# A two-layer transformer stack on one core: the written-out order of every engine redone, the experts' down products two pieces behind in the bank of the turns, and the last batch finished in halves

## The chip, the cores and the metric

The kernel runs on one core of a Trainium2 chip. Its time is the device time of one execution in microseconds (us). The core has five engines with a queue of instructions each: TensorE (PE in the rows; its weight loads are shown apart as PEld), VectorE (DVE), ScalarE (ACT), GpSimd (POOL) and SyncE (SP). An engine executes its queue in order, and waits on semaphores that the others raise. SP issues most of the transfers.

## The reference

The input x is (4, 512, 128) float32: four batches of 512 tokens, width 128. Two layers follow each other:

```
x = L0_attn_x
for L in (0, 1):
    xn = layernorm(x)
    s = attention_L(xn)            # L=0: 16 heads, window of 64, softmax of scores scaled by a "fitness"
                                   # L=1: windows of 64 blended, out projection, then a dense MLP (128-512-128)
    g = silu(experts_L(xn))        # each token goes to one of 8 experts, 128-512-128
    x = x + s * g                  # L=0: erf-gelu between the products; L=1: relu
```

## The kernel before

**What the pieces are.** The attention of a batch is cut into eight units. In layer 0 a unit is first scored (`scores0`), ScalarE takes the tanh of the scores (L906), and VectorE reduces the scores and the tanh (`reduce0`, L1197 and L1200); after the eighth unit the fitness of the batch is known (`inverse`, `inverse_sum`, `fitness`, `turn_fitness`, `spread_fitness`, `fit_q`), and a period later the same units run once more as `logits0`, exp on ScalarE (L915), `weigh0`, `turn_back`, `normalise_head`, `turn_head0`, `project_out`, `keep_out0`. Layer 1 has the same two passes (`scores1`, `reduce1`; `logits1`, `weigh1`, `blend`, `turn_head1`, `project_out`, `keep_out1`), and then the dense MLP (`mlp_stats`, `mlp_norm`, `mlp_turn`, `mlp_up`, `mlp_hidden`, `mlp_down`, `mlp_out`).

**The experts.** The tokens are sorted by expert: GpSimd scatters the rows of `xn` into `sorted_x` in DRAM with 16 indirect transfers (L1456). The sorted rows are 24 tiles of 128, worked in pairs: 12 groups per layer, `g` = 0 to 11 for layer 0 and 12 to 23 for layer 1. Of each group SP loads two blocks of weights and 256 rows (`load`), TensorE transposes the rows into bank ED of `ps_turn` (`pe_turn`), ScalarE copies them out (`act_turn`, L366), TensorE multiplies by the first weights into banks EX and ED (`pe_up`, eight products recorded as 16 instructions, L349), VectorE adds the bias (`vec_bias`, L385), ScalarE applies gelu or relu (`act_hidden`, L371), TensorE multiplies by the second weights (`pe_down`, also 16 instructions, L358), ScalarE copies out (`act_out`, L377), GpSimd adds the bias (`pool_bias`, L392) and SP stores. The weights and rows live in a ring of two groups. When a layer's groups are done, the rows are gathered back (`gather`, L1463), and `join` adds s * g to x.

**What sets the order.** Each engine's program is written out by hand as ten periods of eleven steps. at(p, k) is step k of period p. In period p batch p-1 is scored and batch p-2 is weighed in layer 0, batch p-5 and p-6 likewise in layer 1, and batch p-7 goes through the MLP. `u` is k-3, the unit of the second pass. GROUP_AT says in which step a group is turned and multiplied up. In the step of group g the order was:

- TensorE: `pe_turn(g)`; `logits`, `turn_back`; `scores`; `project_out`; projections of the next batch; `inverse_sum`, `turn_fitness`, `spread_fitness`; `values`; `pe_up(g)`; the MLP; `weigh`, `turn_head`; and in the step after, as its last work, `pe_down(g)` into bank EX.
- ScalarE: `act_turn(g)`; exp; tanh; copies; `act_hidden(g)`; and at the end of the step after, `act_out(g)`.
- VectorE: `normalise_head`/`blend`; `reduce0`/`reduce1`; `keep_out`; the norm of the next batch; the fitness; joins; the MLP; `vec_bias(g)` last.
- SP: `store(g)` two steps after the group's step, and right behind it `load(g + 2)`.

Single PSUM banks are handed on by `Bank.take`: whoever wants bank M (shared by the projections, the values, the spread norms, the turned heads and the MLP) waits on PE until the last holder's result has been read by VectorE or ScalarE. The packing of q and k for a batch (`pack0`, `pack1`, L299) is 12 transfers on SP for q and 12 for k, and that of the fitted q (`pack_fit`) is 18.

## Time and profile before

| | us |
|---|---|
| median of 3 runs | 671.32 (670.61 to 672.29) |
| the profiled execution | 669.64 |
| its span, first to last instruction | 667.8 |
| TensorE busy | 486.0 (73%) |
| VectorE busy | 329.9 (49%) |
| ScalarE busy | 259.6 (39%) |
| GpSimd busy | 125.1 (19%) |
| mean granted TensorE clock | 0.761 of full |

A busy time is the sum of the spans of an engine's instructions. The granted clock is 1.0 at 2.4 GHz and 0.5 at 1.2 GHz; a mean between the two says how the stretch is divided between them.

### The profile page before, as it was taken

How to read it: one execution, taken by the hardware profiler on the slowest of the kernel's cores; microseconds unless marked ns; L12 is line 12 of the kernel's file. 1: busy time of each engine (PE TensorE's matmuls, PEld its weight loads, DVE VectorE, ACT ScalarE, POOL GpSimd, SP SyncE). 2: the span in 40 equal slices, each digit the busy share in tenths (PEclk: the TensorE clock that was granted, in tenths of full speed). 3: DMA queues.
4: the chain of work that ended last, by engine and by line, in shares of the span. 5: the costliest groups of instructions: out<-in, count | busy, mean ns of one | idle time of the engine just before them, and what ended most of it. 6: DMA issues, size and time to landing. Idle time of an engine off the chain costs nothing.

```text
span 667.8 us, 16301 instructions
## 1 busy us (share of the span) xinstructions
PE 486.0 (73%) x6899; PEld 357.2 (53%) x6904; DVE 329.9 (49%) x760; ACT 259.6 (39%) x349; POOL 125.1 (19%) x142
## 2 busy tenths in 40 slices
PE   3844775767676857677679768769998889877835
PEld 2723554646455634434445346547587767764723
DVE  5756855374524664878473567245222623321151
ACT  3114314456544642362143232115641465347112
POOL 6437000000000002132212110711000110027010
PEclk9556788788968886595676665558897999898758
DMA  8631657355722355115452150266323534312010
GB/s 243 165 58 60 214 167 152 104 118 130 158 91 88 98 77 74 19 36 76 72 73 43 27 77 3 65 192 153 97 90 99 162 111 130 95 61 53 14 48 16
DMA packets 49552, 63.57 MB, mean 95 GB/s; under 512 B 9396, under 2 KB 41012, under 8 KB 49460
## 3 DMA queue, kind: packets, MB, share of 16 engines
q1 hardware_dynamic: 46440, 55.97, 35.3%
q0 software_dynamic: 3040, 6.56, 3.8%
q8 instruction: 54, 0.88, 0.6%
q14 instruction: 18, 0.15, 0.1%
HBM read 38.33 MB, written 8.26 MB: 70 GB/s over the span
## 4 chain that ended last, share of the span: by engine, by line
PE 38%; DVE 20%; issue 16%; SPq 9%; ACT 6%; POOL 6%; DMA 5%; ACTq 0%; POOLq 0%; DVEq 0%
SPq L299 6%; POOL sorted_x L1456 4%; PE ps_turn L349 4%; PE ps_turn L358 4%; DMA xg<-sorted_x 4%; PE ps_proj L768 3%; PE ps_proj L617 2%; PE ps_score L697 2%; PE ps_score L760 2%; PE ps_proj L742 2%; DVE tsum L1200 2%; PE ps_proj L610 2%; PE ps_score L725 2%; DVE gm L1197 2%; SPq L326 1%
## 5 line engine op out<-in xcount | busy, mean ns | idle before, releaser
L915 ACT ACTIVATE pT<-ps_score 128x1024 f32<-128x1024 f32 x64 | 65.6, 1025 | 28.6 <-PE ps_score L725 16.4
L392 POOL TENSOR_TENSOR ys<-ys,wblock 128x256 f32<-128x256 f32 x24 | 17.4, 725 | 310.9 <-ACT ys L377 310.9
L1290 DVE TENSOR_REDUCE gm<-ps_score 128x16 f32<-128x1024 f32 x32 | 39.1, 1221 | 63.0 <-PE ps_score L697 62.9
L1197 DVE TENSOR_REDUCE gm<-ps_score 128x8 f32<-128x1024 f32 x32 | 39.1, 1222 | 62.6 <-ACT pT L906 62.5
L358 PE MATMUL ps_turn<-wblock,xn 128*128 128x128 f32 x384 | 57.8, 313 | 12.1 <-ACT xn L371 12.1
L358 PEld LDWEIGHTS ps_turn<-wblock,xn 128*128 128x128 f32 x384 | 54.0, 224 | 17.4 <-ACT xn L371 15.7
L349 PE MATMUL ps_turn<-xgT,wblock 128*128 128x128 f32 x384 | 58.5, 316 | 0.3 <-ACT xgT L366 0.3
L349 PEld LDWEIGHTS ps_turn<-xgT,wblock 128*128 128x128 f32 x384 | 55.3, 229 | 2.6 <-issue 1.7
L371 ACT ACTIVATE xn<-xn 128x1024 f32<-128x1024 f32 x24 | 25.3, 1055 | 58.9 <-DVE xn L385 58.9
L906 ACT ACTIVATE pT<-ps_score 128x1024 f32<-128x1024 f32 x32 | 32.6, 1020 | 39.0 <-PE ps_score L554 38.8
L385 DVE TENSOR_TENSOR xn<-ps_turn,wblock 128x512 f32<-128x512 f32 x48 | 31.9, 685 | 14.7 <-PE ps_turn L349 14.2
L933 ACT ACTIVATE headT<-ps_proj 128x128 f32<-128x128 f32 x32 | 8.8, 276 | 77.0 <-PE ps_proj L631 41.4
L1200 DVE TENSOR_REDUCE tsum<-pT 128x8 f32<-128x1024 f32 x32 | 38.7, 1208 | 0.0
L1309 DVE RECIPROCAL wtot<-ps_proj 128x32 f32<-128x32 f32 x16 | 5.7, 357 | 66.7 <-PE ps_proj L617 66.7
L1456 POOL DMA_INDIRECT sorted_x<-xn,pos x32 | 30.9, 965 | 41.3 <-DVE pos L1152 32.1
L924 ACT ACTIVATE ctxT<-ps_proj 128x512 f32<-128x512 f32 x32 | 19.1, 598 | 43.7 <-PE ps_proj L742 23.5
L610 PE MATMUL ps_proj<-pT,v 128*32 128x256 f32 x256 | 26.4, 489 | 11.3 <-DVE head L1255 11.3
L1463 POOL DMA_INDIRECT moe<-sorted_y,pos x32 | 30.7, 959 | 21.2 <-DMA sorted_y<-ys 12.3
L742 PE MATMUL ps_proj<-pT,v 128*18 128x64 f32 x1024 | 25.4, 249 | 9.5 <-DVE xsT L1313 9.5
L617 PE MATMUL ps_proj<-first,ctxT 128*128 128x128 f32 x128 | 25.6, 332 | 6.5 <-ACT ctxT L924 6.4
L742 PEld LDWEIGHTS ps_proj<-pT,v 128*18 128x18 f32 x1024 | 19.1, 112 | 18.5 <-issue 13.6
L524 PE MATMUL ps_proj<-rmsn,spread 128*128 128x128 f32 x64 | 14.5, 398 | 12.5 <-DVE rmsn L1182 10.6
(294 smaller groups left out, 964.1 us busy)
## 6 DMA issues: line engine op xcount, KB each, us to landing
wblock<-in_L_we SPq DMA_DIRECT2D x48, 578.0 KB, 4.5
qT<-xs SPq DMA_DIRECT2D x48, 64.0 KB
xg<-sorted_x SPq DMA_DIRECT2D x24, 128.0 KB, 5.6
sorted_y<-ys SPq DMA_DIRECT2D x24, 128.0 KB, 1.8
q2raw<-xn SPq DMA_DIRECT2D x48, 64.0 KB
eq<-xs SPq DMA_DIRECT2D x36, 64.0 KB
ek<-xl SPq DMA_DIRECT2D x36, 64.0 KB
sorted_x<-moe POOLq DMA_DIRECT2D x2, 768.0 KB, 8.5
```

The source lines that it names most:

```text
L299: eng.dma_start(dst[r:r + HD, :, :], parts[64 * par:64 * par + 64, s, :]).then_inc(loaded, 16)
L349: ins = te.matmul(bank[:, c * P:(c + 1) * P], w1[:, 2 * (g % 2) + n, c * P:(c + 1) * P], xgT[:, n, :], start=True, stop=True)
L358: ins = te.matmul(EX[:, n * P:(n + 1) * P], hT[:, n, c * P:(c + 1) * P], w2[:, 2 * (g % 2) + n, c * D:(c + 1) * D], start=(c == 0), stop=( ...
L610: ins = te.matmul(o, v0[b % 2][:, u, 32 * g:32 * g + 32], pT[:, n % 2, par * 512 + hf * 256:par * 512 + hf * 256 + 256], start=True, stop= ...
L617: ins = te.transpose(CT[:, j * P:(j + 1) * P], ctxT[:, j * P:(j + 1) * P], ident)
L742: ins = te.matmul(o, v[:, b % 2, m, 18 * h:18 * h + 18], pT[:, n % 2, 64 * h:64 * h + 64], start=True, stop=True)
L906: nc.scalar.activation(th[:, n % 2, :], SLOT[PLACE["p1", 0, b, n]], ACT.Tanh, scale=0.5).then_inc(f.th, 1)
L915: nc.scalar.activation(pT[:, n % 2, :], SLOT[PLACE["p2", L, b, u]], ACT.Exp).then_inc(s.p, 1)
L1197: nc.vector.tensor_reduce(gmx[b % 2][:, t, :].rearrange("p (a r) -> p a r", a=2)[:, :, 4 * hf:4 * hf + 4], SLOT[PLACE["p1", 0, b, n]].rear ...
L1200: nc.vector.tensor_reduce(tsum[:, t, :].rearrange("p (a r) -> p a r", a=2)[:, :, 4 * hf:4 * hf + 4], th[:, n % 2, :].rearrange("p (a j k) ...
L1290: nc.vector.tensor_reduce(gm[:, b % 2, :].rearrange("p (a m r) -> p a m r", a=2, m=NU)[:, :, m, :], SLOT[PLACE["p1", 1, b, m]].rearrange(" ...
L1456: po.indirect_dma_start(out=sorted_x, out_offset=bass.IndirectOffsetOnAxis(ap=pos[:, t:t + 1], axis=0), in_=xn[:, t * D:(t + 1) * D], in_o ...
```

## The change

It changes when each piece of work stands in each engine's queue, and very little of what is computed.

- **Groups of layer 0** stand one place earlier in GROUP_AT: the first at step (1,4) instead of (1,6), the last at (3,4) instead of (3,6). Their first loads are at (1,1) instead of (1,2).
- **Rows and weights** are loaded by two functions with two semaphores. `pe_turn` waits for the rows alone, `pe_up` for the weights. The rows of group g+2 are asked for in the step after group g's, once it is turned; the weights of g+2 three steps after g's step, behind `store(g)`.
- **`pe_down(g)`** moves from the end of the step after to the step two after, right behind `pe_turn(g+1)`, and writes columns 256 to 511 of ED, the bank whose columns 0 to 255 hold the turned rows. `act_turn` now waits for the down product before as well.
- **TensorE's step** becomes: `spread_fitness`; `logits`, `turn_back`; `project_out`; `inverse_sum`, `turn_fitness`, `turn_max`; `pe_turn`; `pe_down`; `scores`; projections; `values` (layer 0's at k = 3 instead of 2); `pe_up`; the MLP; `weigh`, `turn_head`.
- **ScalarE's step**: exp; `act_turn(g)`; `act_out(g-1)`; tanh; copies; and `act_hidden(g)` near the end of the step after.
- **VectorE's step**: `vec_bias` of the step before comes first, then `normalise_head`/`blend`, the norm of the next batch (`mean_square`, `rms_inverse` and `normalise` at k = 3, 4, 5 and 6), `keep_values0`, `split_in`, `mlp_out` (at k = 10 instead of 9), the fitness, `keep_out`, and only then `reduce0`/`reduce1`. The `bn_stats` of the MLP move from `mlp_stats` into `keep_out1`, one with each tile.
- **The end**: the four last tanh stand together at (10,0) and write to `xrT` instead of the single tile `tj`; the joins of layer 1 stand together at (10,4), behind `mlp_norm` of the last batch. Batches 0 to 2 are joined as before. For batch 3 the join is made of what is known before the down product of the MLP, and `last_out` adds that product in two halves, one from bank M and one from EX, each followed by its own output transfer.
- **GpSimd**: `mlp_root` and `mlp_bias` stand ahead of `pool_bias` in their step; the last gathers are two steps later in the list. **SP**: the output transfers stand behind the loop.

The diff, cut to its core:

```diff
-GROUP_AT = [at(1, 6), at(1, 8), at(1, 10), at(2, 1), at(2, 3), at(2, 5), at(2, 7), at(2, 9), at(3, 0), at(3, 2), at(3, 4), at(3, 6),
+GROUP_AT = [at(1, 4), at(1, 6), at(1, 8), at(1, 10), at(2, 1), at(2, 3), at(2, 5), at(2, 7), at(2, 9), at(3, 0), at(3, 2), at(3, 4),
-FIRST_LOADS = {at(1, 2): 0, at(7, 0): 1}
+FIRST_LOADS = {at(1, 1): 0, at(7, 0): 1}
...
             def pe_turn(self, te, g, turn_bank):
-                te.wait_ge(self.loaded[g % 2], 48 * (g // 2 + 1))
+                te.wait_ge(self.rows_in[g % 2], 16 * (g // 2 + 1))
...
                 te.wait_ge(self.kept, g + 1)
+                te.wait_ge(self.loaded[g % 2], 32 * (g // 2 + 1))
...
-            def pe_down(self, te, g, up_bank):
+            def pe_down(self, te, g, turn_bank, beside_turn):
                 te.wait_ge(self.hidden, g + 1)
-                up_bank.take(te, self.y, g + 1)
+                if beside_turn:
+                    turn_bank.held = (self.y, g + 1)
+                else:
+                    turn_bank.take(te, self.y, g + 1)
...
-                        ins = te.matmul(EX[:, n * P:(n + 1) * P], hT[:, n, c * P:(c + 1) * P],
+                        ins = te.matmul(ED[:, (2 + n) * P:(3 + n) * P], hT[:, n, c * P:(c + 1) * P],
...
                     ac.wait_ge(self.up, 2 * g)
+                    ac.wait_ge(self.down, g)
...
+                if c == B - 1:
+                    exb.take(te, m1.out, c + 1)
                 for t in range(NT):
+                    o = (EX if c == B - 1 and t >= 2 else M)[:, t * D:(t + 1) * D]
...
-                    if s in GROUP:
-                        ex.pe_turn(te, GROUP[s], edb)
...
+                    if s in GROUP:
+                        ex.pe_turn(te, GROUP[s], edb)
+                    if s - 2 in GROUP:
+                        ex.pe_down(te, GROUP[s - 2], edb, s in GROUP)
...
-                    if s - 1 in GROUP:
-                        ex.pe_down(te, GROUP[s - 1], exb)
...
-                    if s in GROUP:
-                        ex.act_hidden(ac, GROUP[s])
...
                     if s - 1 in GROUP:
-                        ex.act_out(ac, GROUP[s - 1])
-                    if s in LAST_JOIN:
-                        join_tanh(1, LAST_JOIN[s])
+                        ex.act_hidden(ac, GROUP[s - 1])
+                    if s == at(10, 0):
+                        for n in range(B):
+                            join_tanh(1, n)
...
+            def last_out():
+                for h in range(2):
+                    lo = (B - 1) * T + h * 2 * D
+                    dv.wait_ge(m1.dn, 2 * B - 1 + h)
+                    st(nc.vector.scalar_tensor_tensor(out=s_out[:, lo:lo + 2 * D], in0=(M, EX)[h][:, h * 2 * D:(h + 1) * 2 * D], scalar=0.5,
+                                                      in1=moe[:, lo:lo + 2 * D], op0=ALU.mult, op1=ALU.mult))
+                    nc.vector.tensor_tensor(x[:, lo:lo + 2 * D], x[:, lo:lo + 2 * D], s_out[:, lo:lo + 2 * D], ALU.add).then_inc(j_x, 1)
...
+                    if s - 1 in GROUP:
+                        ex.vec_bias(dv, GROUP[s - 1])
...
-                    if s in GROUP:
-                        ex.vec_bias(dv, GROUP[s])
-                    if s in LAST_JOIN:
-                        join(1, LAST_JOIN[s])
+                    if s == at(10, 4):
+                        for n in range(B):
+                            join(1, n)
+                        last_out()
...
-                    if s - 2 in GROUP:
-                        g = GROUP[s - 2]
+                    if s - 3 in GROUP:
+                        g = GROUP[s - 3]
                         ex.store(sp, g)
                         if g % NG + 2 < NG:
-                            ex.load(sp, g + 2)
+                            ex.load_weights(sp, g + 2)
+                    if s - 1 in GROUP and GROUP[s - 1] % NG + 2 < NG:
+                        g = GROUP[s - 1]
+                        sp.wait_ge(ex.turned, g + 1)
+                        ex.load_rows(sp, g + 2)
```

## Rows read from the trace of the kernel before

**Rows 1.** The page: busy time, share of the span and instructions of each engine.

```profile
PE 486.0 (73%) x6899; PEld 357.2 (53%) x6904; DVE 329.9 (49%) x760; ACT 259.6 (39%) x349; POOL 125.1 (19%) x142
```

**Rows 2.** Busy time by stage: stretch, length, engines, clock, DMA share, GB/s.

```profile
98.00:179.00 81.00, 58.36 (x658) 44.42 (x657) 43.49 (x73) 44.46 (x56) 4.34 (x6) 0.85 0.58 136
179.00:250.00 71.00, 47.85 (x539) 36.26 (x541) 36.05 (x57) 34.84 (x44) 2.89 (x4) 0.85 0.37 90
250.00:321.00 71.00, 50.29 (x538) 28.59 (x535) 49.60 (x117) 26.48 (x35) 18.92 (x17) 0.64 0.37 54
...
480.00:545.00 65.00, 57.86 (x1051) 47.74 (x1044) 25.11 (x53) 26.39 (x41) 5.91 (x7) 0.89 0.39 117
```

**Rows 3.** The waits of TensorE: total us, times, longest.

```profile
PE ps_turn L358 <- ACT xn L371: 12.1, 9, 3.9
PE ps_proj L610 <- DVE head L1255: 11.3, 7, 3.9
PE ps_turn L341 <- DMA xg<-sorted_x: 11.3, 8, 2.7
PE ps_proj L500 <- DVE rmsn L1174: 11.1, 3, 5.2
PE ps_proj L524 <- DVE rmsn L1182: 10.6, 4, 5.2
...
PE ps_proj L742 <- DVE xsT L1313: 9.5, 7, 2.6
...
PE ps_proj L629 <- DVE s_out L1321: 6.1, 4, 2.3
PE ps_proj L495 <- DVE s_out L1262: 5.9, 2, 3.0
```

**Rows 4.** The timeline of period 1: start, us, engine, line, operation [idle before].

```profile
54.91 0.31 PE L500 MATMUL ps_proj<-second,xnT 128*64 128x32 f32 x1 [2.76 <-DVE rmsn L1174]
...
59.53 0.61 PE L542 MATMUL ps_score<-masks 64*128 64x512 bf16 x2
...
64.71 1.49 SPq L327 DMA_DIRECT2D wblock<-in_L_we  x2
...
65.92 2.08 PE L524 MATMUL ps_proj<-rmsn,spread 128*128 128x128 f32 x8 [5.19 <-DVE rmsn L1182]
...
71.90 0.69 PE L341 MATMUL ps_turn<-first,xg 128*128 128x128 f32 x2 [0.77 <-DMA xg<-sorted_x]
```

**Rows 5.** ScalarE's copies of an expert group: busy, mean ns, idle before.

```profile
L366 ACT ACTIVATE xgT<-ps_turn 128x256 f32<-128x256 f32 x24 | 9.2, 382 | 13.5 <-PE ps_turn L341 13.3
```

**Rows 6.** The timeline: the down products of a group, at 1.2 and 2.4 GHz.

```profile
195.31 3.31 PE L358 MATMUL ps_turn<-wblock,xn 128*128 128x128 f32 x16
...
465.28 2.05 PE L358 MATMUL ps_turn<-wblock,xn 128*128 128x128 f32 x16
```

**Rows 7.** The timeline of SP's queue in period 2: one packing of k.

```profile
158.75 8.25 SPq L299 DMA_DIRECT2D v<-xl  x12
```

**Rows 8.** The timeline of the last period.

```profile
639.15 0.77 PE L629 MATMUL ps_proj<-first,xsT 128*128 128x128 f32 x2 [2.31 <-DVE s_out L1321]
...
643.65 0.29 DVE L1321 TENSOR_TENSOR s_out<-s_out,ps_proj 128x128 f32<-128x128 f32 x1
...
646.55 0.87 DVE L1328 BATCH_NORM_STATS2 mstats<-s_out 128x6 f32<-128x128 f32 x4
...
649.20 1.12 DVE L1341 TENSOR_SCALAR sqq<-s_out,mmv,mrstd 128x128 f32<-128x128 f32 x4 [1.17 <-POOL mrstd L1489]
...
658.30 3.84 PE L768 MATMUL ps_proj<-third,q2raw 128*128 128x128 f32 x32 [0.78 <-ACT q2raw L973]
...
664.42 0.69 DVE L1166 SCALAR_TENSOR_TENSOR x<-moe,x 128x512 f32<-128x512 f32 x1
```

**Rows 9.** DMA issues on the page: KB each, median us to landing.

```profile
wblock<-in_L_we SPq DMA_DIRECT2D x48, 578.0 KB, 4.5
...
sorted_y<-ys SPq DMA_DIRECT2D x24, 128.0 KB, 1.8
```

More of the change, by code:

```diff
@@ L315, in __init__ @@
             def __init__(self):
-                self.loaded = [sem(f"x_in_ring{n}") for n in range(2)]
+                self.rows_in = [sem(f"x_rows_in_ring{n}") for n in range(2)]
+                self.loaded = [sem(f"x_weights_in_ring{n}") for n in range(2)]
                 self.turned, self.kept = sem("x_turned"), sem("x_turned_kept")
@@ L992, in scalar_program @@
                         exp(g1, 1, b1 - 1, u)
+                    if s in GROUP:
+                        ex.act_turn(ac, GROUP[s])
+                    if s - 2 in GROUP:
+                        ex.act_out(ac, GROUP[s - 2])
                     if 0 <= b0 < B and k < NU:
@@ L1154, in join @@
             def join(L, c):
-                y, s_, x_ = (z[:, c * T:(c + 1) * T] for z in (moe, s_out, x))
+                y, s_, x_, t_ = (z[:, c * T:(c + 1) * T] for z in (moe, s_out, x, xrT))
                 dv.wait_ge(j_e, B * L + c + 1)
@@ L1321, in keep_out1 @@
                 nc.vector.tensor_tensor(s_out[:, i * D:(i + 1) * D], s_out[:, i * D:(i + 1) * D], M[:, P:2 * P], ALU.add).then_inc(g1.o, 1)
+                dv.wait_ge(g1.o, NT * b + n + 1)
+                st(nc.vector.bn_stats(mstats[:, TILES[n], :], s_out[:, i * D:(i + 1) * D]))
             def mlp_stats(c):
-                dv.wait_ge(g1.o, NT * (c + 1))
-                for t in range(NT):
-                    i = c * NT + t
-                    st.beside(nc.vector.bn_stats(mstats[:, t, :], s_out[:, i * D:(i + 1) * D]))
-                st.meet()
                 for t in range(NT):
@@ L1394, in vector_program @@
                         keep_out1(b1 - 2, 1 + k)
[L1395 to L1414 removed]
+                    if 0 <= b0 < B and k == 9:
+                        turned_fitness(b0)
+                    if 0 <= b0 - 2 < B and k == 0:
+                        normalise_head(b0 - 2, 3)
+                    if 0 <= b1 - 2 < B and k == 0:
+                        blend(b1 - 2, 3)
+                    if 0 <= b0 < B and k < NU:
+                        reduce0(b0, k)
+                    if 0 <= b1 < B and k < NU:
+                        reduce1(b1, k)
+                    if 0 <= b0 < B and k == 7:
+                        inverse(b0)
                     for n in range(B):
@@ L1520, in gpsimd_program @@
                     s = at(p, k)
[L1521 to L1523 removed]
+                    if 0 <= c < B and k == 3:
+                        mlp_root(c)
+                        mlp_bias(c)
+                    if s - 2 in GROUP:
+                        ex.pool_bias(po, GROUP[s - 2])
+                    if s - 3 == GROUP_AT[NG - 1]:
                         gather(0, 0)
```

172 lines of the change are left out of this document (81 added, 91 removed).

## The prediction

> **What bounds the kernel now.** I read the page's busy shares first: TensorE is busy for 73% of the span, VectorE for 49%, ScalarE for 39% [rows 1]. No engine is full, so the question is what the fullest one waits for. The busy time by stage, cut where the periods begin, says where: in periods 2 to 4 of layer 0, 98 to 321 us, TensorE is busy for 58.4 + 47.9 + 50.3 = 156.5 of 223 us, and in 480 to 545 us, where layer 1's experts run, for 57.9 of 65 [rows 2]. Layer 0 is a lockstep of queues with some 30% of slack on TensorE; layer 1's expert stage is near TensorE's bound, and little is to be had there.
>
> The table of waits then says on what [rows 3]. The reader should see three families. (a) Results of VectorE that are short but stand in its queue behind work that is itself waiting: the rms norm (11.1 and 10.6 us) and the sum into `s_out` (6.1 and 5.9), together 33.7 us. (b) The head and blend normalisation, 11.3 + 9.5 = 20.8 us. (c) The experts' own chain: 12.1 us for the gelu or relu before the down product, 11.3 us for rows from DRAM.
>
> Two ends remain. At the front the experts can't start before the scatter has landed: SP issues the first loads at 64.7, and the first turn is at 71.9 [rows 4]. At the back, TensorE has only the last batch's chain to carry, so everything between 632 us and the end counts in full [rows 8].
>
> **The change part by part.** All sums are made against the profiled execution, 669.64 us, which lies 1.7 below the median of 671.32.
>
> *1. VectorE's short results ahead of the reduces, and TensorE's readers of them later.* In the old order `mean_square`, `rms_inverse` and `keep_out` wait in line behind a reduce that waits for the tanh of the same step. In the new order they are done in that idle time. The instructions are the same; what goes is the wait. Of the 33.7 us I take off 2.8 + 5.2 = 8.0 that lie in period 1 [rows 4], since that period is bound by other things (point 5). Of the 25.7 left TensorE saves at least nothing and at most all. I take 22: the result moves forward by a whole reduce pair and `values0` a step back, more than any single wait of this family is long (5.2 at most). The smaller rows of the same kind are left out of the sum, as a reserve. Bounds: 8 to 26.
>
> *2. Head and blend ahead of the norm and the reduces.* 20.8 us of waits. Here the input itself comes late, through context copy and `turn_back`, so only VectorE's own queue time goes, and `vec_bias` now stands in front of it. I take 9; bounds 0 to 20.
>
> *3. Down product two steps behind, rows apart.* The down product has a full step more for bias and gelu: of 12.1 us I take 9. The rows no longer wait for two blocks of weights (578 KB in all, 4.5 us to landing, [rows 9]): of 11.3 us I take 6, because the first rows of each layer still wait for the scatter. Bounds for both together: 5 to 23.
>
> *4. The end.* The first joins of layer 1 stand in VectorE's queue ahead of the sum that TensorE needs. At 639.15 TensorE has waited 2.31 us for that sum, which itself takes 0.29; with 0.1 of handing over, 1.9 us are the join's, and the second join costs the same. The third stands between the last sum, which ends at 643.94, and the statistics at 646.55, 2.6 us. All three go, 6.4 us. One `bn_stats` of the four remains in the chain: three quarters of 0.87, 0.6 us. The last piece now: the MLP's down products end at 658.30 + 3.84 = 662.14, then four VectorE operations of 0.69 run until 665.1. After: two operations on half the width behind the second half, some 0.4 each with 0.1 of handing over (an estimate from half the 0.69), so 663.1: 2.0 us less. The cover for the four joins moved to (10,4): 12 operations of 0.69 and a step of 0.03, 8.7 us, start where `mlp_norm` ends at 650.3 and are done at 659.0, before 662.1; without that cover they would cost up to 3 us. In all 9; bounds 6 to 10. [rows 8]
>
> *5. What it costs at the front.* The old queue reached `scores0` of step 4 at 59.5 us [rows 4]. The new one has `pe_turn(0)` in front of it, and everything in TensorE's queue behind waits: scores, norm spreads, the next reduces. The rows are issued from 64.7; a transfer of the same 128 KB to DRAM took 1.8 us [rows 9], the old mix of rows and weights about 7 (64.7 to 71.9). So the scores of step 4 start between 67 and 72, 8 to 12 us later than before. Given back: the old 5.19 us stall behind them falls into it, and one group more is finished when period 2 starts, worth two times 2.05 us of products and a turn. Step by step I come to period 2 starting 6 to 8 us later with 4.5 us more work done. Net cost 4; bounds 0 to 9.
>
> *6. New waits in the expert chain.* `act_turn(g)` now waits for `pe_down(g-1)`, which is queued behind the turn, and `pe_up(g)` waits for the copy. Where scores stand between, this is covered. It is bare in the eight groups whose step has no scores: (1,8), (1,10), (2,9), (7,8), (7,10), (8,9), (9,0), (9,2). Price: two copies of 0.382 [rows 5] and 0.1 of handing over, 0.9 each: 7 us; bounds 2 to 15, the upper one if a further operation of ScalarE stands in front as well. A rule of the Trainium skill bears on it. The row shows copies of 0.38 us and nothing of what would happen without the wait. The page "PSUM — Partial Sum Buffer", section "PSUM bank collisions raise a hardware error", says that semaphores must guard a bank and not an address, since two engines at disjoint columns of one bank collide; by it the wait can't be dropped and turns and down products in one bank always pay it. No run here shows a collision.
>
> *7. Weights behind the packing.* The weights of g+2 are asked for behind `store(g)`, now a step later, and SP executes in order. In period 2 the two packings stand at steps 6 and 7, 8.25 us each [rows 7], and the weights for step 9 behind them; in period 1 the same for step 10. From the down product that frees their place: 16.5 us of packing, some 6 for two stores and their issues (two weight issues alone take 1.49, [rows 4]), 4.5 to landing [rows 9], 27 in all. They are needed four steps later: 81 us over 11 steps are 7.4 each now [rows 2], some 5.8 if the forecast holds, 23 in all. That is 4 us late each. I take 5 for both; bounds 0 to 10.
>
> *Sum.* -22 - 9 - 9 - 6 - 9 = -55; +4 + 7 + 5 = +16; -39. Of the 46 us of points 1 to 3, I let 7 come back as waits for whatever is late next (ScalarE's table loads between exp and gelu, the fit of a batch before its second pass, neither moved earlier): -32. That gives 637.6 for a profiled execution, and about 638 as a median, one for the difference to it.
>
> **The rivals.**
>
> *A. The clock adds to it.* In 98 to 321 us the granted clock is 0.85, 0.85 and 0.64 [rows 2], a mean of 0.78, so some 43% of that time is at 1.2 GHz, where sixteen products take 3.31 us and not 2.05 [rows 6]. If the removed waits bring the mean to 0.90 (20% at the lower level), then 23% of 156.5 us of work, 36 us, runs at the higher one and takes 2.05/3.31 of its time: 14 us more gained, 624. For it: the low levels lie in the stretches with gaps. Against it: period 4 and 5 have no experts and stay thin. The Trainium skill, "TensorE: Matmul & The Clock Gate", section "HAM oscillation — how this bites in real kernels", has it that idle gaps are what throws the clock back; the trace agrees in that 480 to 545, the fullest stretch, has 0.89.
>
> *B. The waits re-form.* TensorE is spared a wait only to stand at the next one: what VectorE delivers earlier was late only because its inputs were. Then points 1 to 3 give 23 instead of 46, the costs 16 stay, the end gives 9: -16, about 655. For it: half of family (b) and (c) has its cause upstream. Against it: the norm's waits come from VectorE's queue alone.
>
> *C. Slower, by bunching.* Turn, down and up now stand in one step, 4.5 us of dense work, and the step between has only small products. If that costs the clock, the stretches with experts (81 + 71 us at 0.85, 65 us at 0.89) fall. Each 0.01 of mean clock there is 2% of the time moved to 1.2 GHz: 2% of 217 us with some 75% busy, 3.3 us of work, slowed by a factor of 1.6 from the higher level, 2.0 us more. A fall of 0.16, to the level of 0.7, costs 32 us and cancels the forecast; a fall to 0.64, as in period 4, costs about 43, and the time is 682. It decides from a clock of 0.69. Against it: the even steps were thin before too.
>
> *D. No difference*: the costs 5 to 7 at their upper bounds (34 us) against half of the gain. About 670.
>
> **How the numbers follow.** Forecast 0.50, A 0.18, B 0.17, C 0.10, D 0.05. The likeliest one's own range is 624 to 652: the costs at their lower bounds (2 in all) give -14, those of points 1 to 3 at a third less give +15. The range of 8 in 10 runs from 610 (A, with points 1 to 3 near their upper bounds) to 666 (B with costs above what I take); it leaves out C, most of D, and a small part of A. This kernel can't be told from no change within 0.3%, 2 us. Faster by more than that: the forecast, A and nearly all of B, 0.84. Within: 0.05. Slower: 0.11.
>
> **What would show it.** Point 1: the waits L500 and L524 for `rmsn` and L495 and L629 for `s_out` fall from 33.7 to about 12. Point 2: those of L610 and L742 fall from 20.8 to about 12. Point 3: L358 behind ScalarE below 3, rows below 5. Point 4: from the last projection's sum to the end some 9 us shorter; the last output transfer issued within 1 us of the end of the down products. Point 5: a wait of 7 us or more at `pe_turn(0)`, and period 2 starting at 104 or later and not at 98. Point 6: a new wait of `pe_up` for the copy, some 7 us in all. Point 7: `pe_up` of (1,10) and (2,9) waiting for weights. A: mean clock above 0.80. The prediction is wrong if the waits reappear under other names with the same sum (B), or if the clock in 100 to 250 us falls below 0.75 (C).

## The result, and the profile after

The changed kernel takes 652.96 us in the median of four runs (646.74 to 656.53), the kernel before, beside it on the same chip, 671.58 (670.61 to 672.29). It is 18.6 us faster, where 33 were forecast. The ratio is 0.969, with a 95% interval from 0.962 to 0.976; ratios with an interval, here and below, count only the runs within 1.5% of the shortest of their kernel (here all but 656.53), and so differ a little from those of the medians (0.972 here). 652.96 lies inside the range of 610 to 666 and just outside the forecast's own range of 624 to 652. The profiled execution is the longest of the four, 656.53 with a span of 654.7; its granted clock is 0.758, that of the shortest 0.778.

The page's busy times come first, against [rows 1]. TensorE does the same 6,900 products.

```profile
PE 493.6 (75%) x6904; PEld 362.5 (55%) x6904; DVE 334.1 (51%) x763; ACT 256.2 (39%) x347; POOL 126.2 (19%) x142
```

It is busy for 7.6 us longer than before, with no more work: more of it ran at the lower clock. The idle time of TensorE fell by 20.7 us, and so the span by 13.1. Where that went is in the table of TensorE's waits (engine, what is written, line, what is waited for; then us in total, times, longest), against [rows 3]:

```profile
PE ps_turn L353 <- issue: 20.3, 6, 6.5
PE ps_turn L366 <- ACT xn L380: 18.6, 15, 2.5
PE ps_proj L569 <- DVE inv L1244: 12.3, 4, 5.4
PE ps_turn L344 <- DMA xg<-sorted_x: 11.1, 2, 7.5
PE ps_proj L751 <- DVE xsT L1338: 9.5, 7, 2.6
...
PE ps_score L594 <- DMA q2raw<-xn: 8.2, 2, 6.7
...
PE ps_proj L619 <- DVE head L1280: 5.3, 6, 1.3
...
PE ps_turn L353 <- ACT xgT L375: 3.4, 7, 0.6
...
PE ps_proj L509 <- DVE rmsn L1199: 2.1, 1, 2.1
...
PE ps_proj L638 <- DVE s_out L1346: 0.9, 2, 0.5
...
PE ps_proj L533 <- DVE rmsn L1207: 0.4, 1, 0.4
```

The lines have moved: L500, L524 and L629 of before are L509, L533 and L638; the head's products L610 are L619, and L742 is L751; turn, up and down product of the experts, L341, L349 and L358, are L344, L353 and L366. The wait of L495 for `s_out` is gone from the list. So the 33.7 us of short VectorE results have become 3.4, more than forecast, though the same lines now wait 4.7 us for other results of VectorE, `v` (2.3) and `xsT` (2.4). The four rows of the experts (L353 twice, L366, L344) are 53.4 us together, where the same waits were 23.7 before. The reader should then look at the first two rows. The biggest wait now is that of the up product. It is put down to "issue", which means that no engine's signal ended it; what was missing is seen in the order of events. Up (L353) needs the copied rows and the weights, and the copy's own wait stands apart (L375, 3.4 us). The queues around the longest of these waits, 6.54 us, in the order of time: TensorE, GpSimd (POOL) and SP.

```profile
506.78 2.05 PE L366 MATMUL ps_turn<-wblock,xn 128*128 128x128 f32 x16 [1.40 <-ACT xn L380]
```

```profile
511.07 1.02 POOL L1514 TENSOR_TENSOR mrstd<-mvar,neghalf 128x4 f32<-128x4 f32 x1 [10.70 <-DVE mvar L1355]
...
515.10 1.27 POOL L1519 TENSOR_TENSOR s_out<-s_out,third 128x512 f32<-128x512 f32 x1 [3.02 <-DVE sqq L1363]
...
516.33 0.72 POOL L401 TENSOR_TENSOR ys<-ys,wblock 128x256 f32<-128x256 f32 x1
...
517.08 0.38 SPq L337 DMA_DIRECT2D sorted_y<-ys  x1
518.21 1.48 SPq L332 DMA_DIRECT2D wblock<-in_L_we  x2
```

```profile
525.48 3.71 PE L353 MATMUL ps_turn<-xgT,wblock 128*128 128x128 f32 x16 [6.54 <-issue]
```

The down product of group (8,1) ends at 508.83. Its weights' place is free once GpSimd has added `b2` to the copied result (L401), and that comes at 516.33 only: the MLP's root and bias of step (8,3) were moved ahead of it, and each waits for VectorE. Behind L401 stand the store, and the loads of group (8,5) at 518.21, whose up product starts 7.3 us later; a load takes 5.4 us to landing in the median of this kernel (4.5 before, [rows 9]), and these took up to 6.1. At 175.49 us, the group of (2,9), TensorE waits 4.00 us, and there it is SP's packings that stand in front of the weights: GpSimd's bias is done at 159.30, the last packing is issued at 167.13. At 110.52, the group of (1,10), it waits 3.67 us for another reason: the packing was issued by 97.90, before the bias was done (99.73), and the weights, asked for from 101.13, took up to 8.2 us to land.

The front went as described, and further. TensorE stands at the first turn for 7.52 us and at the first up product for 2.67 more:

```profile
65.83 0.69 PE L344 MATMUL ps_turn<-first,xg 128*128 128x128 f32 x2 [7.52 <-DMA xg<-sorted_x]
72.32 3.75 PE L353 MATMUL ps_turn<-xgT,wblock 128*128 128x128 f32 x16 [2.67 <-issue]
```

In layer 0, ScalarE's first tanh of period 2 was at 101.43 us and is now at 115.98, 14.6 us later. Its last tanh of period 4 was at 295.18, and is now at 282.94, 12.2 earlier: periods 2 to 4 gave 26.8 us, a few of which are the one expert group that now runs before them. The exp that was at 528.19, early in layer 1's expert stage, is at 506.75, 21.4 earlier. But the exp of 592.72 is at 587.42, only 5.3 earlier. A stretch with the same TensorE work in both kernels shows it (length; busy us and instructions of each engine; clock, DMA share, GB/s), first after, then before:

```profile
505.00:590.00 85.00, 67.86 (x1144) 55.65 (x1141) 25.49 (x61) 33.99 (x49) 7.60 (x9) 0.88 0.31 97
```

```profile
526.00:595.00 69.00, 60.62 (x1146) 49.74 (x1145) 24.15 (x61) 32.38 (x48) 6.63 (x8) 0.98 0.38 112
```

1,145 instructions took 69 us and take 85. Of the 16 us, 7.2 are the clock (0.98 and now 0.88 for the same products), and 8.8 are idle time: the 6.5 at 525.48, and the down product's wait for its activation (relu in this layer), which in this stretch is 5.1 us in five places and was 1.5 in two. The idle time comes again on another chip (the next section); the lower clock does not. Between the same two exps, the 49th and the 57th of 64, it was 0.97 before and 0.87 after on the first chip, 64.5 and 80.7 us apart. In the experiments the changed kernel takes 77.7 us for this stretch at 0.91, and beside it on the same chip the kernel with the old experts' chain takes 67.0 at 0.90.

How the clock fell is seen in shorter pieces of the same stretch:

```profile
505.00:515.00 10.00, 8.14 (x220) 6.78 (x216) 5.20 (x13) 5.30 (x8) 1.02 (x1) 1.00 0.23 71
515.00:525.00 10.00, 2.98 (x74) 2.47 (x60) 1.24 (x2) 3.12 (x5) 2.67 (x3) 0.86 0.56 175
525.00:530.00 5.00, 4.52 (x52) 4.39 (x52) 1.39 (x2) 0.34 (x1) 0.00 (x0) 0.60 0.63 234
...
560.00:575.00 15.00, 13.66 (x228) 11.72 (x228) 2.69 (x8) 3.99 (x7) 0.26 (x1) 0.77 0.28 84
```

It was full until 515. In the ten us with the long wait TensorE was busy for 3.0, and behind it the sixteen up products ran at 0.60, in 3.71 us and not 2.05. At 560 to 575 it is low again, with no such gap before it (TensorE was busy for 13.3 of the 15 us from 545): not all of the 7.2 us hang on the wait, and by the other chip's figures they need not hang on the change.

The end came out as worked out [rows 8]. From the last exp (626.07 before, 622.30 after) to the end of the span it took 41.7 us and takes 32.4, 9.3 less. The last rows after:

```profile
639.67 1.11 PE L760 MATMUL ps_proj<-first,sqq 128*128 128x128 f32 x4 [3.69 <-DVE sqq L1363]
...
648.46 0.69 DVE L1179 SCALAR_TENSOR_TENSOR x<-s_out,x 128x512 f32<-128x512 f32 x1
...
649.61 1.95 PE L780 MATMUL ps_turn<-third,q2raw 128*128 128x128 f32 x16
...
651.60 0.42 DVE L1190 SCALAR_TENSOR_TENSOR s_out<-ps_turn,moe 128x256 f32<-128x256 f32 x1 [0.83 <-PE ps_turn L780]
652.05 0.42 DVE L1192 TENSOR_TENSOR x<-x,s_out 128x256 f32<-128x256 f32 x1
```

The four joins end at 649.15, before the down products (651.56), and two half-width operations of 0.42 follow: the cover held. The last output transfer is issued at 652.51, within 1 us of the down products' end, as said.

### The profile page after: what moved, and what is told of

Its sections match the earlier page's. It is cut to its first block, busy times and chain, and to the rows that moved or that the text cites. A ratio compares the mean times of both kernels' runs of the same rounds, so it can differ in the third digit from the quotient of the medians.

```text
span 654.7 us, 16294 instructions
## 1 busy us (share of the span) xinstructions
PE 493.6 (75%) x6904; PEld 362.5 (55%) x6904; DVE 334.1 (51%) x763; ACT 256.2 (39%) x347; POOL 126.2 (19%) x142
## 4 chain that ended last, share of the span: by engine, by line
PE 48%; DVE 16%; ACT 11%; issue 10%; SPq 5%; POOL 5%; DMA 4%; ACTq 0%; DVEq 0%; POOLq 0%
PE ps_turn L366 8%; PE ps_turn L353 7%; SPq L298 5%; POOL sorted_x L1481 4%; ACT xn L380 3%; PE ps_proj L780 2%; PE ps_score L769 2%; PE ps_proj L751 2%; PE ps_proj L619 2%; PE ps_proj L626 2%; PE ps_score L706 2%; DMA q2raw<-xn 2%; PE ps_score L734 2%; PE ps_proj L533 2%; ACT pT L918 2%
## 5 line engine op out<-in xcount | busy, mean ns | idle before, releaser
L927 ACT ACTIVATE pT<-ps_score 128x1024 f32<-128x1024 f32 x64 | 65.6, 1024 | 58.0 <-PE ps_score L734 29.6
L366 PE MATMUL ps_turn<-wblock,xn 128*128 128x128 f32 x384 | 65.3, 340 | 18.6 <-ACT xn L380 18.6
L353 PE MATMUL ps_turn<-xgT,wblock 128*128 128x128 f32 x384 | 59.8, 320 | 23.9 <-issue 20.3
L366 PEld LDWEIGHTS ps_turn<-wblock,xn 128*128 128x128 f32 x384 | 61.3, 251 | 22.9 <-ACT xn L380 22.8
L401 POOL TENSOR_TENSOR ys<-ys,wblock 128x256 f32<-128x256 f32 x24 | 17.9, 747 | 277.4 <-ACT ys L386 277.4
L353 PEld LDWEIGHTS ps_turn<-xgT,wblock 128*128 128x128 f32 x384 | 55.4, 229 | 28.2 <-issue 22.8
L1334 DVE RECIPROCAL wtot<-ps_proj 128x32 f32<-128x32 f32 x16 | 5.7, 358 | 64.5 <-PE ps_proj L626 64.5
L375 ACT ACTIVATE xgT<-ps_turn 128x256 f32<-128x256 f32 x24 | 9.2, 384 | 64.2 <-PE ps_turn L366 51.8
L751 PE MATMUL ps_proj<-pT,v 128*18 128x64 f32 x1024 | 26.0, 253 | 9.5 <-DVE xsT L1338 9.5
L619 PE MATMUL ps_proj<-pT,v 128*32 128x256 f32 x256 | 27.5, 506 | 5.4 <-DVE head L1280 5.3
L751 PEld LDWEIGHTS ps_proj<-pT,v 128*18 128x18 f32 x1024 | 19.5, 114 | 18.2 <-issue 14.3
```

Of the source, the lines that this page charges most:

```text
L353: ins = te.matmul(bank[:, c * P:(c + 1) * P], w1[:, 2 * (g % 2) + n, c * P:(c + 1) * P], xgT[:, n, :], start=True, stop=True)
L366: ins = te.matmul(ED[:, (2 + n) * P:(3 + n) * P], hT[:, n, c * P:(c + 1) * P], w2[:, 2 * (g % 2) + n, c * D:(c + 1) * D], start=(c == 0), ...
L619: ins = te.matmul(o, v0[b % 2][:, u, 32 * g:32 * g + 32], pT[:, n % 2, par * 512 + hf * 256:par * 512 + hf * 256 + 256], start=True, stop= ...
L751: ins = te.matmul(o, v[:, b % 2, m, 18 * h:18 * h + 18], pT[:, n % 2, 64 * h:64 * h + 64], start=True, stop=True)
L927: nc.scalar.activation(pT[:, n % 2, :], SLOT[PLACE["p2", L, b, u]], ACT.Exp).then_inc(s.p, 1)
```

## The experiments

They ran on four other chips, one group of kernels on each, and there the kernel before takes 725 to 732 us, not 671 (more on this below). So a kernel is compared with the kernels of its own group, or by its ratio to the kernel before. Kernels of different groups are on different chips, and differences between their medians are rough.

| kernel | median us | before, same chip | ratio, 95% interval |
|---|---|---|---|
| end alone | 723.5 | 727.0 | 0.995 (0.991 to 0.999) |
| old chain | 681.9 | 727.0 | 0.937 (0.930 to 0.944) |
| old places | 691.8 | 727.0 | 0.945 (0.937 to 0.952) |
| relu for gelu | 690.6 | 727.0 | 0.952 (0.947 to 0.958) |
| changed kernel | 692.5 | 728.8 | 0.950 from the medians |
| old chain, again | 681.0 | 728.8 | 0.937 (0.931 to 0.942) |
| old places, again | 697.3 | 728.8 | 0.949 (0.939 to 0.959) |
| weights in two | 678.1 | 728.8 | 0.934 (0.929 to 0.940) |
| one wait | 730.0 | 725.0 | 1.013 (1.006 to 1.020) |
| orders alone | 688.5 | 725.0 | 0.953 (0.947 to 0.960) |
| old chain, weights in two | 670.9 | 725.0 | 0.927 (0.920 to 0.934) |
| own bank | 684.2 | 731.6 | 0.945 (0.939 to 0.951) |

**The changed kernel again.** No edit.

> The changed kernel itself once more, beside those of this group on one chip, since the chip of the first experiments ran the kernel before in 727 us and not in 671. Theory: its ratio to the kernel before is a property of the kernel and comes out at 0.962 to 0.976 on any chip. Rival: the ratio depends on the chip, because TensorE there also waits for its own instructions ('issue' waits in mid-product), and an order with other waits hides them otherwise: then it differs from 0.969 by over 0.01.

It took 681.5 to 696.0 us in six runs, five of them over 692; since none of the five is within 1.5% of the shortest, no interval is given for its ratio. By the medians it is 0.950, where the first chip gives 0.972. The rival holds as far as this goes: the ratio hangs on the chip.

**Old places.** Layer 0's groups stand where they stood.

```
-GROUP_AT = [at(1, 4), at(1, 6), ... at(3, 2), at(3, 4),
+GROUP_AT = [at(1, 6), at(1, 8), ... at(3, 4), at(3, 6),
```

> The changed kernel with one thing put back: layer 0's twelve expert groups at steps (1,6) to (3,6), as before, not (1,4) to (3,4). All else as changed (median 653, period 2 starting at 114 us). Theory F, the first group stands too early: its turn waits 7.5 us for rows and its up product 2.7 for weights, with period 1's scores queued behind; then that wait falls below 2 us, period 2 starts at 106 or earlier, and the time is 643 to 648. Rival G: what period 1 saves is paid by the group that now ends two steps later in period 3, and the time stays at 650 to 656.

> The changed kernel with layer 0's groups at the old places (1,6) to (3,6), again, beside the changed kernel on one chip. Theory F (the first group stands too early and costs period 1 some 8 to 12 us): 5 to 10 us less than the changed kernel. Rival G (what period 1 saves is paid in period 3): within 3 us.

691.8 and 697.3 us, beside 692.5 of the changed kernel. Theory F fails on these chips, but they can't try it: here TensorE stands for 9.2 us in period 1 in any case (below), and when it reaches the first turn in the changed kernel, at 71.64 us, the rows are there and it doesn't wait. What the early first group costs where that halt is missing stays open; the rows above show 10.2 us of waits in front of everything of steps 4 and on.

**The end alone**, on the kernel before: joins at (10,4), `bn_stats` behind each sum, down products and output in halves.

```
+                    if s == at(10, 4):
+                        for n in range(B):
+                            join(1, n)
+                        last_out()
```

> The kernel before with the end alone changed: layer 1's joins at (10,4) instead of (10,0) to (10,2), their tanh in xrT, bn_stats right behind each sum into s_out, the last down products in two banks and the last output in halves. The prediction's point 4 gives -9 (-6 to -10): 661 to 665. Rival: most of the joins' time was covered by other waits, and only the two us of the last piece are gained: 668 to 670.

723.5 against 727.0; by the ratio 3.9 us, 0.8 to 6.9, less than the prediction's 9 and in between the two expectations. Its trace shows more: from the last exp to the end it takes 34.0 us, and 41.7 are what the old end takes, both in the kernel before on the first chip and in orders alone on another.

**Orders alone**: the kernel before, with the orders of norm, heads, sums and values redone on TensorE and VectorE, experts' chain and end as before; the first loads at (1,1) and GpSimd's two MLP steps ahead of its bias came along from the change. In VectorE's step:

```
-                        if k == 2:
-                            mean_square(b0 + 1)
...
+                        if k == 3:
+                            mean_square(b0 + 1)
...
+                    if 0 <= b0 < B and k < NU:
+                        reduce0(b0, k)
```

> The kernel before with the orders of norm, heads, sums and values on TensorE and VectorE redone as in the change, and nothing else: the experts' chain and the end are as before. With the end it took 681. If the end is worth the 9 us of the prediction, this one is at 690; if it is worth what it gave on the kernel before (727.0 to 723.5, some 4), at 685. By points 1 and 2 of the prediction the orders alone are worth 31 us of 727: 696. Rival: they are worth over 40, 687 or less.

688.5, a ratio of 0.953: 34 us of 727 (29 to 39), close to the 31 of points 1 and 2. Its waits for `rmsn` are what the edit was to remove; 11.1 and 10.6 before, on the first chip [rows 3]:

```profile
PE ps_proj L500 <- DVE rmsn L1173: 1.2, 1, 1.2
...
PE ps_proj L524 <- DVE rmsn L1181: 0.5, 1, 0.5
```

The longest wait is now that of the turn for its rows and weights, 22.4 us in six places (11.3 in eight in the kernel before, first chip).

**Old chain**: the changed kernel with the experts' part put back: one load of rows and weights, down products one step behind in their own bank, bias and gelu in the group's own step, old places.

```
-                    if s - 2 in GROUP:
-                        ex.pe_down(te, GROUP[s - 2], edb, s in GROUP)
...
+                    if s - 1 in GROUP:
+                        ex.pe_down(te, GROUP[s - 1], exb)
...
-                            ex.load_weights(sp, g + 2)
+                            ex.load(sp, g + 2)
```

> The changed kernel with the experts' chain put back as before: one load for rows and weights, down products one step behind and in their own bank, gelu and bias in the group's own step, turn first in the step, places (1,6) to (3,6). What is left of the change is the order of norm, heads, sums and values on the engines, and the end. By the prediction's points 3, 5, 6 and 7 the experts' part is worth -15 + 4 + 7 + 5 = +1, so this kernel is at 650 to 656. Theory H, the experts' part costs (its new waits of 18.6 us for gelu, 20.3 for weights and 7.5 for the first rows): 640 to 648. Rival I, the experts' part carries the gain made in periods 2 to 4, and the order of the rest gives little beside the end: 658 to 665.

> The changed kernel with the experts' chain and places as before, again, beside the changed kernel on one chip. Its ratio was 0.937. Theory H (the experts' part of the change costs time): it is at least 1% under the changed kernel here too. Rival: the earlier ratio came from the chip, and the two are within 0.5% of each other.

681.9 and 681.0 us, the latter 11.5 under the changed kernel of its group: theory H. The experts' part of the change costs. Every run of the old chain there (678.2 to 684.3) lies below five of the six of the changed kernel; the sixth, 681.5, is as short as they are, so the size is less sure than the direction. The traces say where it is paid: the two profiled executions are 10.9 us apart, and 10.7 of it lies between the 49th and the 57th exp, in layer 1's expert stage (77.7 and 67.0 us). There the changed kernel waits 6.7 us at the same up product as on the first chip and 3.8 for the hidden activation, where the old chain has neither wait. The waits put down to "issue", of which these chips have more, hardly differ: without those at the up product they are 49 us in the changed kernel and 53 in the old chain, and none of them is in that stretch.

Against orders alone (0.953) the old chain (0.937) has the end besides, which is then worth 0.017 of 727, 12 us with an uncertainty of some 6. In the traces it is 8: from the last exp to the end 41.7 us in orders alone, 33.7 in the old chain and in the changed kernel of this group.

**Relu for gelu.** The changed kernel; it leaves out the real gelu of layer 0's experts.

```
-                nc.scalar.activation(h_, h_, ACT.Gelu if g < NG else ACT.Relu)
+                nc.scalar.activation(h_, h_, ACT.Relu)
```

> The changed kernel with layer 0's gelu of the experts replaced by relu (it leaves out the real gelu), which shares a table with exp and tanh, so that some 24 table loads of 1.28 us go from ScalarE. The down product of layer 0 waits 18.6 us for the gelu in the changed kernel. Theory T, the loads are what makes it late: the wait falls below 7 us and the time is 640 to 646. Rival V, the bias of VectorE or ScalarE's queue itself is late: the wait stays above 13 us and the time is 649 or more.

690.6: nothing gained that can be told, although 13 table loads of 1.28 us are gone (7 at the gelu, 6 of the 14 at the exp), not the 24 that I had put down. The down product's wait fell from 18.6 (changed kernel, another of the four chips) only to 11.3, so most of it isn't the loads, and the 7.3 us that it lost seem to be paid elsewhere: the up product's wait for weights stands at 26.0 here, 20.4 in the changed kernel. Rival V is nearer, though its figure for the wait is missed too.

```profile
PE ps_turn L353 <- issue: 26.0, 5, 8.3
...
PE ps_turn L366 <- ACT xn L380: 11.3, 10, 2.1
```

**Weights in two**: the changed kernel; the up product's weights are asked for one step behind the group's turn, the down product's as before.

```
                         sp.wait_ge(ex.turned, g + 1)
                         ex.load_rows(sp, g + 2)
+                        sp.wait_ge(ex.biased, 2 * g + 2)
+                        ex.load_weights(sp, g + 2, 0)
...
```

> The changed kernel with each expert's weights in two transfers: those of the up product are asked for in the step after the group's turn, as soon as the bias has read the old ones, those of the down product where all of them were before. The up product waits 20.3 us for weights in the changed kernel, in 6 places. If these waits were on the path: below 8 us left, and 6 to 12 us less than the changed kernel. Rival: the wait moves to the down product's weights or to the packing, which now stands behind more issues on SP: within 3 us of the changed kernel.

678.1 us, 14.4 less than the changed kernel of its group, more than expected. In the two profiled executions TensorE is busy equally long (491.6 and 491.9 us), so what went is idle time; the stretch between the 49th and the 57th exp takes 71.1 us and not 77.7. The row of 20.4 us of the changed kernel (first) is gone; the up product waits for the copy alone (second):

```profile
PE ps_turn L353 <- issue: 20.4, 5, 6.8
```

```profile
PE ps_turn L371 <- ACT xn L385: 14.9, 12, 2.1
...
PE ps_score L600 <- DMA q2raw<-xn: 12.4, 3, 5.6
...
PE ps_turn L357 <- ACT xgT L380: 4.9, 11, 0.6
```

**One wait**: the changed kernel, the turn waiting for both transfers.

```
                 te.wait_ge(self.rows_in[g % 2], 16 * (g // 2 + 1))
+                te.wait_ge(self.loaded[g % 2], 32 * (g // 2 + 1))
```

> The changed kernel (median 692) with one thing undone: the turn waits for rows and weights, as before, and not for rows alone. The prediction takes 6 us for rows apart: 696 to 700. Theory M: since the rows of the next group are asked for behind the same late weights on the same queue, nothing is gained by turning early and the up product waits instead: 691 to 694, with the 20 us of waits at the up product now at the turn, where the scores of the step stand behind them too. Rival N: these scores make it cost more than predicted, 704 or more.

730.0 us, some 40 more than the changed kernel on another chip (37.5 by the medians, 41 by their ratios to the kernel before): rival N, and far beyond it. Its TensorE waits:

```profile
PE ps_turn L345 <- issue: 44.3, 11, 9.8
...
PE ps_turn L345 <- DMA wblock<-in_L_we: 8.1, 2, 4.8
```

The weights are late in 13 of the places, 52.4 us in all, where the changed kernel waits 20.4 at the up product; the work between turn and up, the scores of the same step above all, covers the rest. Not all of these 32 us are lost: the wait for the gelu falls from 18.6 to 5.9 meanwhile. In the two profiled executions, 34 us apart, TensorE idles 23 us longer, and is busy 11 longer at a clock of 0.731 and not 0.758. With the new orders and the old chain the turn's wait for rows and weights is 18.8 us (old chain) and 22.4 (orders alone). So "rows apart" is worth much more here than the 6 us that I gave it, and most of what it hides is a lateness that the change itself makes, by storing and reloading a step later.

**Old chain, weights in two**: the two edits together.

> The kernel with the experts' chain as before (median 681) and the transfers cut finer: rows of group g+2 asked for as soon as group g is turned, the up product's weights as soon as the bias has read the old ones, the down product's weights behind the store. Against the changed kernel with its weights in two (median 678) it differs in the chain alone: down product one step behind in its own bank, gelu in the group's own step. By the prediction the two steps behind and the copy's new wait are worth -9 + 7 = -2: this kernel at 678 to 683. Theory K, the new chain costs also without its waits for weights (each copy waits for a down product, each down product for a gelu two queues away): 668 to 674. Rival L, the new chain gains in earnest once the weights are in time: 685 or more.

670.9 us, 0.927: the best kernel of the study, 54 us under the kernel before of its chip and, by the ratios, 7 under the old chain. Theory K's figure. Against weights in two with the new chain (0.934) it is 0.0076 lower, 5.5 us, but the intervals overlap: that the new chain costs also without its waits for weights is likely, not shown.

**Own bank**: weights in two, down products two steps behind but in EX, so that no copy waits for them; bias and gelu in the group's own step.

```
-                    ac.wait_ge(self.down, g)
...
-                        ins = te.matmul(ED[:, (2 + n) * P:(3 + n) * P], hT
+                        ins = te.matmul(EX[:, n * P:(n + 1) * P], hT
```

> The changed kernel with its weights in two (median 678), and the down product two steps behind as in the change, but in the bank EX of its own as before, so that the copy of the turned rows waits for no down product; bias and gelu stand again in the group's own step, so that the down product finds them done. Theory K (it is the shared bank and the gelu a step later that cost): the down product's wait for the gelu falls from 14.9 us to under 5, and the time is 660 to 668, under the 671 of the old chain with the same transfers, where that wait is 14.5. Rival O: the bias and gelu in their own step delay VectorE's reduces and ScalarE's next tanh by as much: 670 to 680.

684.2 us, 0.945, against 0.934 for weights in two on another chip. The two intervals touch (0.939 to 0.951, 0.929 to 0.940), so slower is likely and not shown; what is shown is that nothing was gained, although the wait for the gelu is gone, from 14.9 to 0.5, as theory K has it. What stands there now:

```profile
PE ps_score L596 <- DMA q2raw<-xn: 14.0, 3, 8.4
PE ps_proj L571 <- DVE inv L1246: 13.6, 3, 10.1
...
PE ps_proj L646 <- ACT headT L947: 9.8, 14, 2.6
...
PE ps_score L596 <- ACT pT L929: 5.7, 5, 1.9
PE ps_turn L357 <- ACT ys L387: 4.7, 11, 0.6
...
PE ps_turn L368 <- ACT xn L381: 0.5, 1, 0.5
```

Weights in two had 12.4, 13.2, 4.4 and 1.1 us in the first four, so the waits that grew are above all those for ScalarE's exp and its copy of the head, behind the gelu that now stands in the group's own step; the inverses and the packing grew by 2 us together. The fifth row is new: in bank EX the up product waits for ScalarE to copy the down product out, 4.7 us, where it waited 4.9 for the copy of the rows. Rival O in its size; its mechanism, of ScalarE rather than VectorE, is an argument from these rows, and wasn't isolated. Against old chain, weights in two (0.920 to 0.934) the intervals are clear of each other: with the weights in time, and without the shared bank and the late gelu, the down product two steps behind and what hangs on it (store and down weights a step later, other places in the step, layer 0's groups two steps earlier) still cost, 0.018 or some 13 us.

## Why the prediction was right, and where its sum was off

The direction and its main cause were right. Some 15 us of the forecast gain did not come: the orders and the end gave near what was said, and the experts' part was costed far too low.

*Point 1 and 2, orders: right.* Forecast 31 us; alone they gave 34 (29 to 39) on the other chips. On the first chip the waits of (a) fell from 33.7 to 3.4, where I said 12, and those of (b) from 20.8 to 14.8, where I said 12. The 7 us that I let come back without a row have one: TensorE, earlier than before, now stands 8.2 us in two places for the packing of the fitted q (L594), and its wait for the inverse (L569) rose from 8.0 to 12.3, 12.5 us together.

*Point 4, the end: right in the trace* (9.3 for 9), with the joins covered as worked out. The two comparisons of kernels lie on either side of it, 3.9 on the old order and some 12 on the new; their traces have 8. The sign for it was set at the wrong place: from the last projection's sum it is 5.5 us less (24.15 and 18.60 to the end), since two of the joins stood ahead of that sum.

*Point 3, the experts' chain: wrong.* I took 9 off the down product's wait for its input. It rose from 12.1 to 18.6. The step behind was given to the chain and taken away at once, since bias and gelu went a step back as well: the gelu now stands near the end of ScalarE's queue of the step before. At 211.83 TensorE has waited 2.51 us for it, and ScalarE's rows show why; a root for the norm and its table load go first:

```profile
206.77 1.02 ACT L918 ACTIVATE pT<-ps_score 128x1024 f32<-128x1024 f32 x1
207.80 1.28 ACT L911 ACT_TABLE_LOAD   x1
209.10 0.31 ACT L911 ACTIVATE rmsn<-rmsn 128x128 f32<-128x128 f32 x1
209.42 1.28 ACT L380 ACT_TABLE_LOAD   x1
210.72 1.06 ACT L380 ACTIVATE xn<-xn 128x1024 f32<-128x1024 f32 x1
```

Of the 11.3 us for rows I took 6 off; they are 11.1, in two places, the first groups of the two layers (7.52 and 3.58). Elsewhere the rows are in time; the two first ones alone are over the 5 that I allowed in all. I had also misread [rows 9]: the 578 KB are one block of weights and not two, so a group loads 1156 KB; the 4.5 us to landing are those of one block's transfer.

*Point 7, weights: the term that failed most.* I took 5 us, for two groups that stand behind packings. The waits are 20.3 in six places, and taking them away gave 14 on another chip. I had read the later store as a matter of SP's queue in two spots, and waits of the size came there (3.67 and 4.00 us for "4 us late each"). Only the second came by the way described; that the first fits is luck, since there the packing was out of the way and the weights took up to 8.2 us to land, not 4.5. And the later store delays every group's weights by a step, as one wait shows (52 us at the turns). The longest wait has by the trace a cause that I hadn't read in the diff at all: GpSimd's two MLP steps ahead of `pool_bias`, which was free to start from 509.89, when the down product had been copied, and started at 516.33. No run put these steps back alone. That wait lies in layer 1's expert stage, which I had set aside as "near TensorE's bound".

*Point 6, the copy: right in its row* (3.4 us in 7 waits, where 7 in 8 were said). The wait for the down product shows rather in ScalarE's queue, where the copy stood for 51.8 us in 18 places. On the page of the Trainium skill "PSUM — Partial Sum Buffer" (section "PSUM bank collisions raise a hardware error"), by which a shared bank needs that wait: no run here left it out, and with the down product in its own bank another wait of the same size took its place (4.7 for 4.9 us) and nothing was gained.

*Point 5, the front.* The wait of 7 us came (7.52), and period 2 started 14.6 us later, not 6 to 8. The old 5.19 us stall did fall into the new wait, but period 1 has others behind it: 2.67 and 3.67 us of up products waiting for weights, and 5.42 of `inverse_sum` (L569) for VectorE's inverse, 1.50 before. The net cost of the front wasn't measured.

*The rivals.* A didn't happen: the clock is 0.758, not above 0.80, with TensorE idle for 20.7 us less. Its argument that the low levels lie in the stretches with gaps was thin in [rows 2] already, where 179 to 250 us has TensorE busy for 67% at 0.85, and 250 to 321 for 71% at 0.64. The sign set for C, a clock below 0.75 in 100 to 250 us, did not come: it is 0.85 there, as before. A lower clock was seen in one stage only, 0.98 to 0.88 in layer 1's expert stage, for 7.2 us, and not again on another chip (0.91 beside 0.90 for the old chain). Part of it is a fall behind the gap of 6.54 us, where the trace agrees with the Trainium skill's "TensorE: Matmul & The Clock Gate" (section "HAM oscillation — how this bites in real kernels"), by which idle gaps throw the clock back; the fall at 560 us has no such gap ahead of it. B, waits that re-form, is the best name for what took nearly half of the gain: the experts' waits rose by 30 us, from 23.7 to 53.4, and the fit's packing and inverse by 12.5, while the norm's are gone.

Put together, in 727 us: orders -34, end -8 to -12 (with the old chain 0.937, -46), the experts' part some +10 by the medians, the changed kernel some -36. On the first chip it is -19 to -21 of 671; how its parts divide there was not measured by experiment.

## What to carry to other kernels

Short results that another engine waits for belong ahead of long reductions that are themselves waiting: that reorder alone was worth 5% on the chip where it was tried. Before a consumer is moved a step later, follow what its end releases over all queues: here GpSimd's bias, the store, and behind it the reload of the same buffer, so every group's weights. And when two edits come together, ask whether one only hides the other's cost: the separate semaphore, put down for 6 us, was worth some 40, most of it as a cover for lateness that its companions had made.

## What the hardware showed that I had not expected

The kernel before takes 671 us on one chip and 725 to 732 on four others. ScalarE's 64 exps take 65.6 us in both, so the engine is no slower at its work. TensorE has more idle time in the middle of products, put down to "issue". For the products of L734 (weight loads and matmuls together) the row of the changed kernel is, first on the first chip, then on another:

```profile
  issue: 8.5, 32
```

```profile
  issue: 71.5, 93
```

And in period 1 of that other chip TensorE finishes its sixteen products (L563) at 53.34 us and stands until 62.52 for ScalarE's `sqk`. ScalarE itself had stood for 10.68 us, which the profile puts down to no engine of the core ("remote"), ahead of a tanh whose scores were done at 48.3:

```profile
60.20 1.02 ACT L918 ACTIVATE pT<-ps_score 128x1024 f32<-128x1024 f32 x1 [10.68 <-remote]
```

```profile
62.52 0.65 PE L522 MATMUL ps_proj<-sqq,first 128*32 128x128 f32 x8 [9.19 <-ACT sqk L907]
```

This falls in the time of the scatter. That the instructions themselves arrive late would fit, but no run tried it. It does show that one and the same order can be worth 3% on one chip and 5% on the next.
